# GpSimd's double product of a recurrence as four instructions of 256 columns in place of one of 1024

## The reference

```python
def _L0_attn_ref(x, lmlg, theta, last_conv_init):
    gamma = jnp.exp(-jnp.exp(lmlg))
    c = gamma * jnp.exp(1j * theta)
    filt = c[None, :] ** n                       # n = 0, 1, 2, ...
    ...                                          # causal convolution of x with filt, by FFT
    conv_with_past = conv_filter_x + last_conv[None] * filt[:, None] * c
    return conv_with_past.real * x

x = _layernorm(x + _L0_attn_ref(x, ...))         # recurrence along the 32 sequences
x = _layernorm(x + _L0_xattn_ref(x, ctx, ctx, ...))   # 16 heads of 16 channels, 256 keys
x = _layernorm(x + _L0_ffn_ref(x, ...))          # nearest of 8 centroids picks the expert of a token
```

## Time and profile before

| | us |
|---|---|
| median of 3 runs (1237.98 to 1245.02) | 1239.13 |
| the profiled execution | 1245.21 |
| its span, first to last instruction | 1243.4 |
| PE, DVE, ACT, POOL busy in the span | 1110.6, 955.3, 668.9, 775.6 |
| full steps: 26 double products of GpSimd | from 117.43 to 704.32 |

### The profile page before, as it was taken

How to read it: one execution, slowest core, us unless ns; L and a number is a source line. 1 busy time by engine, 2 the same in 40 slices (tenths; PEclk the granted TensorE clock), 3 DMA queues, 4 the chain that set the end, 5 groups by cost and what they waited for, 6 DMA issues and landing times.

```text
span 1243.4 us, 27486 instructions
## 1 busy us (share of the span) xinstructions
PE 1110.6 (89%) x8030; PEld 818.2 (66%) x8061; DVE 955.3 (77%) x2416; ACT 668.9 (54%) x1416; POOL 775.6 (62%) x932
## 2 busy tenths in 40 slices
PE   3899989999999999989999998853999999999996
PEld 2566666666666666656666666532888888888885
DVE  7458988999989999999999998845555555555553
ACT  4257666767767767767767767541222222222221
POOL 4646879889979888978978955450333333333333
PEclk9679999999999999999999998656999999999998
DMA  4667667766556556556556554042111111111110
GB/s 128 162 162 205 178 179 208 188 148 161 148 134 163 142 142 163 147 138 163 144 141 163 134 130 109 11 153 60 48 51 48 43 51 51 50 47 49 50 52 19
DMA packets 90825, 144.91 MB, mean 117 GB/s; under 512 B 12662, under 2 KB 78335, under 8 KB 84512
## 3 DMA queue, kind: packets, MB, share of 16 engines
q1 hardware_dynamic: 83616, 126.09, 39.2%
q0 software_dynamic: 6528, 16.99, 4.7%
q10 hardware_dynamic: 576, 0.53, 0.2%
HBM read 91.44 MB, written 53.03 MB: 116 GB/s over the span
## 4 chain that ended last, share of the span: by engine, by line
PE 42%; DVE 33%; issue 9%; DMA 6%; POOL 6%; SPq 2%; ACT 1%; POOLq 0%; DVEq 0%; ACTq 0%
DVE neg_max_sb L1312 12%; PE Y L454 10%; PE G L422 8%; PE A L422 8%; DVE oq L1443 4%; DVE u L1335 3%; PE S L1078 3%; DMA neg_max<-nm_row 3%; PE GT L432 2%; PE O L1027 2%; POOL buckets L775 2%; PE M L1035 2%; POOL state L731 2%; DVE st L1296 2%; DVE stx L1296 2%
## 5 line engine op out<-in xcount | busy, mean ns | idle before, releaser
L1312 DVE TENSOR_REDUCE neg_max_sb<-S 128x2 f32<-128x512 f32 x512 | 327.5, 681 | 46.9 <-PE S L1078 46.1
L909 ACT ACTIVATE probs<-T 128x512 f32<-128x512 f32 x512 | 278.1, 595 | 141.0 <-PE T L1091 127.7
L1078 PE MATMUL S<-k_st,q_st 48*128 48x256 f32 x1024 | 215.0, 319 | 38.0 <-DVE neg_max_sb L1312 34.9
L1078 PEld LDWEIGHTS S<-k_st,q_st 48*128 48x128 f32 x1024 | 146.3, 192 | 115.4 <-issue 77.1
L1091 PE MATMUL T<-q_st,k_st 49*128 49x256 f32 x1024 | 211.3, 319 | 6.3 <-DMA q_st<-neg_max 2.6
L1091 PEld LDWEIGHTS T<-q_st,k_st 49*128 49x128 f32 x1024 | 146.4, 192 | 22.8 <-ACT probs L909 15.4
L399 ACT ACTIVATE gT<-GT 128x512 f32<-128x512 f32 x71 | 42.5, 598 | 207.8 <-PE GT L432 207.8
L1027 PE MATMUL O<-probs,v_aug 128*32 128x256 f32 x2048 | 145.6, 404 | 0.8 <-ACT probs L909 0.7
L378 POOL DMA_INDIRECT out<-res,token x71 | 76.5, 1077 | 103.3 <-DVE res L503 98.8
L454 PE MATMUL Y<-dn_sb,gT 128*128 x568 | 134.2, 379 | 0.8 <-ACT gT L399 0.8
L454 PEld LDWEIGHTS Y<-dn_sb,gT 128*128 128x128 f32 x568 | 107.5, 189 | 18.2 <-issue 1.0
(11 more groups left out here) (185 smaller groups left out, 2553.9 us busy)
## 6 DMA issues: line engine op xcount, KB each, us to landing
k_st<-k_pieces SPq DMA_DIRECT2D x64, 256.0 KB, 5.1
q_st<-q_pieces SPq DMA_DIRECT2D x64, 256.0 KB, 3.9
xr<-buckets SPq DMA_DIRECT2D x71, 129.0 KB, 2.1
xt<-in_x SPq DMA_DIRECT2D x32, 256.0 KB, 6.1
ct<-in_ctx SPq DMA_DIRECT2D x32, 256.0 KB, 6.8
k_pieces<-k_hi SPq DMA_DIRECT2D x32, 256.0 KB, 3.6
k_pieces<-k_lo SPq DMA_DIRECT2D x32, 256.0 KB, 3.7
q_pieces<-q_hi SPq DMA_DIRECT2D x32, 256.0 KB, 2.1
```

What stands on the lines that cost most here:

```text
L909: a_.activation(probs[:, h % 8].rearrange("p k t -> p (k t)"), T_ps[h % 2][:, :], ACT.Exp, scale=DH ** -0.5).then_inc(s["exp_ok"], 1)
L1078: last = t_.matmul(S_ps[h % 2][:, c * TOK:(c + 1) * TOK], q_st[base:base + STACK, h, c * P:(c + 1) * P], k_st[base:base + STACK, h, :], st ...
L1312: v.tensor_reduce(neg_max[:, cur.mod(2), :, h], S_ps[h % 2][:, :].rearrange("p (c t) -> p c t", c=NTC), AX.X, ALU.max, negate=True).then_i ...
```

## The change

The one GpSimd product over both rows of `decay` and both halves of the tokens, in which two operands are repeated by broadcasting, becomes a loop of four products of 256 columns without broadcasting. They compute the same numbers into the same places. The waits ahead of them are the same, and the semaphore is raised by the last of the four.

```diff
-                both = [P, 2, NTC, C]
                 re_b = decay_re.unsqueeze(1).to_broadcast([P, NTC, C])
-                pair_b = decay[:, :, :].unsqueeze(2).to_broadcast(both)
 ...
-                    g.tensor_tensor(by_re[:, :, :, :], state[:, 0].unsqueeze(1).to_broadcast(both), pair_b, ALU.mult).then_inc(s["conv"], 1)
+                    for w in range(2):
+                        for c in range(NTC):
+                            last = g.tensor_tensor(by_re[:, w, c], state[:, 0, c], decay[:, w], ALU.mult)
+                    last.then_inc(s["conv"], 1)
```

## The result

The changed kernel takes 1261.92 us (median of 4 runs, 1257.32 to 1266.18), the kernel before 1240.74 us on the same chip: a ratio of 1.0167 (95% interval 1.0126 to 1.0209). It is slower, as forecast, but by 21 us where 9 were forecast, and its time lies above the top of the range, 1257. The profiled execution took 1266.18 us, its span is 1264.3. In the changed kernel the lines behind L705 carry a number higher by one: the offset is L786, `u` L1336, the distances L1462, the second query add L1444, `onehot` L1479, the key cut L795.

A forecast was written before the change was run, and what follows sets the result against it. GpSimd's loop from double product through offset, DVE's distances and slots, and scatter was taken to set the step, with `u` beside it; 22 steps x 0.41 us = 9.0 us on the median 1239.13 gave 1248, range 1239 to 1257.

The forecast's parts named there:

- Pieces: GpSimd's double product, once per step: four pieces of 0.684 us take 2.74 instead of 2.33, adding 0.41 us.
- the term of 9.0 us: Full pipeline steps: 22 steps at 0.41 us more on GpSimd's path to the offset make 9.0 us; chance 0.60.
- `u`: DVE instruction beside the product: would end at about 1.3 us instead of 2.92, lengthening piece two by 0.46 instead of `xw`.
- The rival that no gap opens: Four products hold the way to memory until the last ends; `u` lasts 2.9 us, time again 1248; chance 0.08.
- The lag behind the offset is a release: DVE's distances start 0.33 to 0.37 us behind GpSimd's offset because they wait for it; `u`'s freed time becomes waiting.
- The rival by which they count, 1221: DVE's freed time shortens steps by 0.8 us, 18 us over 22 steps, giving 1221; chance 0.08.
- Covers: Work said to stay hidden: ScalarE's squares, over 0.88 us ahead of the offset, move with `xw` and stay hidden.
- The five products before the pipeline is full: Double products at 19 to 87 us, where GpSimd idles: costed at nothing; without that cover, 2 us more.
- The ties: Two races behind the offset, variance add against query add (0.34 us) and `onehot` against key cut (1.05): same mix forecast.
- the key cut's tie: Whether DVE's `onehot` goes ahead of GpSimd's key cut (0.17 us) or waits it out (1.27), costing 1.05 us.
- a draw of 3 us: Chance variation in how the two ties fall in the bound steps, taken to move the time by some 3 us.
- races fall otherwise: Rival on the two ties: all won 14 us less, all lost 17 more; chance 0.10, for the better, 1234 to 1243.

The follow-up runs named there:

- both ties set: Key cut waits for `onehot`, DVE's first query add for GpSimd's variance add: kernel before so changed 1232.29 us (0.9916), changed kernel (four pieces) 1234.36 us (0.9924).
- the fivefold offset: Kernel before (one product), with the offset's 16-column instruction issued four times more into a spare tile: 1277.25 us (1.0299).
- the two pairs of runs that set it: One product and four: key cut waiting for `onehot`, 1238.02 and 1242.74 us; with DVE's first query add also waiting for the variance add, 1232.29 and 1234.36.
- a hold of DVE to its old time: Changed kernel (four pieces), with DVE's `u` also waiting for the third piece from the sixth item on: 1256.76 us (1.0099).

## Why the prediction was right in direction and wrong in size

*Pieces.* Right. Forecast: 0.684 us a piece, 2.74 for four, 0.41 more. In the run in which `u` came behind them, four undisturbed pieces and `xw` lie 509.28 - 506.52 = 2.76 us apart; the offset is 0.42 to 0.43 later; bound steps with both ties set are 0.43 longer. So the term of 9.0 us held in the last 20 steps (464.02 - 455.00). The Trainium skill ("GPSIMD Engine Reference", section 3.1), by whose figures I estimated 60 ns as the fixed part and 0.18 us a step, isn't borne out in this: the traces show 0.14 us an instruction.

*`u`.* Right: 0.90 us, ended at 1.3, and a piece lengthened in place of `xw`: the four and `xw` are 533.66 - 530.45 = 3.21 us apart, 0.45 above 2.76 (0.46 forecast), and `xw` is back at 1.19. The rival that no gap opens is refuted. The Trainium skill ("SBUF — State Buffer", section "SBUF: two separate sides") calls the pair that DVE and GpSimd share a lock held for the whole instruction; the trace agrees (`u` takes 0.90 us beside four pieces, 2.51 beside one), and shows that it is let go between pieces with nothing to wait for.

*The lag behind the offset is a release.* Right: 0.33 to 0.37 us still, with 0.91 us of idle time ahead of it. The freed 1.6 us bring no distances earlier. The rival by which they count, 1221, is refuted. That all of the 1.6 us would be waiting ahead of the distances was not right: about half of it goes into waiting for TensorE's scores two pairs of maxima earlier.

*Covers.* The squares end 1.1 us ahead of the offset, at 535.94 + 0.19 = 536.13; they stayed hidden, as said:

```profile
535.94 0.19 ACT L975 ACTIVATION_READ_ACCUMULATOR junk<-xw,row 128x1 f32 x1
```

The five products before the pipeline is full were put at nothing; the first full product comes at 115.73 us in place of 117.43, and in the nine other traces with four pieces it comes earlier still.

*The ties.* Wrong, and this is the step that failed: "both fall behind the offset, so their phase is kept and I forecast the same mix". The times of the two engines behind the offset are indeed the same within 0.1 us (`onehot` 4.68 us behind it before and 4.60 after, in steps that lose both ties), but the outcome of the tie isn't a function of those: 23 of 26 steps lost the key cut's tie, in place of 10. It goes one way in nearly all steps where DVE stands idle ahead of the distances and is mixed where DVE comes just in time. Step by step, over the eleven traces that keep GpSimd's order and leave this tie open: 140 of the 146 steps with more than 0.3 us of idle time there lose it, and 61 of the 140 others. With the offset ahead of the query cut, 17 and 24 of 26 lose without any idle time there, so the sign is good for one order only. I had that idle time in the forecast, even as a sign to look for, and gave it no price. What I called a draw of 3 us was worth 9.5 in the last 20 steps. The term that was mis-sized is the rival's: "races fall otherwise" stood in the text with all lost at 17 us, and had 0.10, all of it for the better. With that term in the sum, 1239 + 9 + 17 = 1265, the time is near what came out, 1262.

*What remains open.* That a longer path at which DVE has to wait turns the tie is shown by the fivefold offset; that the tie's loss makes up the rest of the time is shown by the two pairs of runs that set it. By what the waiting, or the lead of TensorE and ScalarE that goes with it, turns the tie, isn't shown: neither the keys' readiness at the key cut nor the place of `nm_row` is it, a hold of DVE to its old time turned it back in the one execution that was traced, and I found no earlier difference between steps that win and lose.

## What to carry to other kernels

When two engines that exclude each other reach the same point within a few hundredths of a us, don't carry the mix of outcomes over to the changed kernel: price it with all won and with all lost, and give "all lost" a real chance whenever the change makes one of the engines wait where it came just in time before. Better, set such ties with a wait: two waits here were worth 10 us, and took away most of what the change cost. Splitting an instruction on the engine whose order sets the loop costs a fixed part per piece at once. Here it returned nothing in the full steps, as the one that was held up by it, `u`, stood beside the loop; that it would pay with `u` on the loop, no run here shows.

## What the hardware showed that was not expected

- An additional GpSimd product costs 0.14 to 0.15 us by itself (offset at 6.40, 6.54 and 6.82 us with one, two and four instructions), and a 16-column one 0.17 us from start to start (four in 0.69).
- An instruction of 16 columns on DVE with two SBUF operands waits as long as a large one: `onehot` 1.24 us instead of 0.15 to 0.19.
- A wait that makes GpSimd idle 0.70 to 0.85 us ahead of its key cut makes the step some 1 us shorter than a lost tie: the key cut then takes 1.28 us instead of 1.68, so GpSimd is hardly later, and DVE isn't held at all.
- With the order left open, the same kernel's bound steps fall into four lengths, 22.69, 22.96, 23.75 (a single step) and 24.09 us (medians before the change), by the two ties alone.
